# Mixer's feature products, K's sums and ScalarE's settling steps in another order, and a finer signal for the gathers

## The reference

```
q, k, v = feat @ Wq, feat @ Wk, feat @ Wv            # N x 4 heads x 64
e = (k[src] * q[dst]).sum(-1) / 16                   # for each edge and head
ft2 = segment_sum(v[src] * softmax_over_dst(e), dst)

qn, kn = normalize(q') * (scale * temperature), normalize(k') * scale    # 8 heads x 32
vN = concat([1, v']) / N
kv_mod = einsum('bhni,bhnj,bhne->bhije', kn, kn, vN)
kv, vsum = einsum('bhnd,bhne->bhde', kn, vN), vN.sum(-2)
y = 0.5 * einsum('bhni,bhnj,bhije->bhne', qn, qn, kv_mod) + scale**2 * (qn @ kv) + scale**4 * vsum
out = (y[..., 1:] / y[..., :1]) @ Wproj.T + bproj
```

## Time and profile before

| | us |
|---|---|
| median of 3 runs | 2665.03 |
| lowest and highest | 2663.69, 2670.76 |
| the profiled execution | 2674.8 |
| its span, first to last instruction | 2673.1 |
| mean granted share of TensorE's clock | 0.845 |
| edges and mixer, about | 110 to 1800 |

### The profile page before, as it was taken

How to read it: one execution, slowest core, us unless ns; L and a number is a source line. 1 busy time by engine, 2 the same in 40 slices (tenths; PEclk the granted TensorE clock), 3 DMA queues, 4 the chain that set the end, 5 groups by cost and what they waited for, 6 DMA issues and landing times. The chain is left out here.

```text
span 2673.1 us, 45626 instructions
## 1 busy us (share of the span) xinstructions
PE 2071.7 (78%) x12642; PEld 1468.3 (55%) x12642; DVE 1745.4 (65%) x3439; ACT 1496.3 (56%) x4918; POOL 1213.7 (45%) x1183
## 2 busy tenths in 40 slices
PE   7757767678767657777777777765989986999998
PEld 4323332223323245555555555544778875999997
DVE  7367676767667675566666656676989996444443
ACT  2256556566556535565665655665875544555554
POOL 0455555555565545455455545542840001444443
PEclk9878788888888857788777777786999997999999
DMA  7666566666665655566556556545950017322221
GB/s 214 207 193 187 171 182 181 188 182 183 190 191 169 188 152 170 173 177 182 171 174 187 168 166 189 175 148 174 312 161 23 31 34 258 69 33 35 33 35 22
DMA packets 227731, 406.06 MB, mean 152 GB/s; under 512 B 58972, under 2 KB 129809, under 8 KB 227521
## 3 DMA queue, kind: packets, MB, share of 16 engines
q0 software_dynamic: 83712, 250.84, 33.7%
q1 hardware_dynamic: 120852, 116.88, 14.7%
q10 hardware_dynamic: 22957, 35.95, 3.7%
HBM read 345.66 MB, written 58.83 MB: 151 GB/s over the span
## 5 line engine op out<-in xcount | busy, mean ns | idle before, releaser
L825 POOL DMA_INDIRECT ring<-kv_tab,idx x904 | 915.4, 1013 | 769.5 <-ACT val L1160 449.8
L1160 ACT ACTIVATE val<-ring,val 128x64 f32<-128x64 f32 x1808 | 475.5, 336 | 15.5 <-DVE part L927 5.9
L921 DVE TENSOR_TENSOR val<-val 128x1040 f32<-128x1040 f32 x113 | 140.4, 1242 | 294.4 <-ACT val L1160 284.8
L884 DVE TENSOR_TENSOR ring<-ring,tile_bank 128x1024 f32<-128x1024 f32 x226 | 273.9, 1212 | 27.5 <-ACT tile_bank L1150 23.4
L1275 PE MATMUL tile_bank<-q_win,spread 128*128 128x256 f32 x452 | 180.7, 487 | 114.5 <-DVE val L913 68.9
L889 DVE TENSOR_REDUCE score<-ring 128x16 f32<-128x1024 f32 x226 | 267.7, 1208 | 0.0
L1308 PE MATMUL bank_f<-pair,u_T 96*125 96x496 bf16 x200 | 94.3, 471 | 180.7 <-ACT u_T L697 55.0
L2226 POOL DMA_INDIRECT out<-e_yw,to_row x56 | 120.8, 2157 | 222.0 <-DVE e_yw L2253 205.6
L2302 PE MATMUL e_h<-e_xT,e_now 128*128 128x128 f32 x1792 | 211.8, 277 | 0.7 <-DVE e_now L2243 0.7
L2302 PEld LDWEIGHTS e_h<-e_xT,e_now 128*128 128x128 f32 x1792 | 207.0, 194 | 1.2 <-DVE e_now L2243 1.1
L1308 PEld LDWEIGHTS bank_f<-pair,u_T 96*125 96x125 bf16 x200 | 29.4, 147 | 322.6 <-issue 122.0
(11 more groups left out here) (423 smaller groups left out, 4956.3 us busy)
## 6 DMA issues: line engine op xcount, KB each, us to landing
g_ring<-parts SPq DMA_DIRECT2D x137, 260.0 KB, 4.3
parts<-part ACTq DMA_DIRECT2D x113, 260.0 KB
q_win<-q_tab SPq DMA_DIRECT2D x226, 128.0 KB
e_w_all<-L_ffn_W SPq DMA_DIRECT2D x16, 1024.0 KB, 11.7
ring<-kv_tab,idx POOLq DMA_INDIRECT x904
kv_tab<-kv_t SPq DMA_DIRECT2D x25, 224.0 KB
blocks<-t SPq DMA_DIRECT2D x216, 5.0 KB
blocks<-t SPq DMA_DIRECT2D x216, 0.0 KB
```

The source lines that it names most:

```text
L825: pool.indirect_dma_start(out=ring[:, n % RING, g * L + e, :], out_offset=None, in_=t.kv_tab, in_offset=bass.IndirectOffsetOnAxis(ap=idx[n ...
L884: dve.tensor_tensor(k, k, bcast(q_ps[g].unsqueeze(1), 128, L, F), ALU.mult).then_inc(q_read[g], 1)
L921: dve.tensor_tensor(v[:, :, 0:2 * FD], v[:, :, 0:2 * FD], v[:, :, 2 * FD:], ALU.add).then_inc(folding, 1)
L1160: one = act.activation(val[n % 2][:, 1, e, h, 0:DG], ring[:, n % RING, L + e, F + h * DG:F + (h + 1) * DG], ACT.Copy, scale=val[n % 2][:, ...
```

## The change

1. TensorE, feature products. k_first and q_first are renamed k_pairs and q_pairs and issued at the end of the micro step before, behind k_last or q_last. K's product gets a second PSUM tile (bank_f2), and waits for the square of head k - 2 where it waited for that of head k - 1.
2. K's sums. The Gram product leaves PSUM accumulation: each half of K (128 columns) is multiplied with V and with itself into one tile of bank_t, and VectorE adds both parts into SBUF (slv_acc and gram_sum). The order of the sums becomes ones, K squared, first half, second half, at k = 0, 2, 4, 5 on TensorE and 1, 3, 5, 6 on VectorE.
3. ScalarE's order. settle_rows moves from the end of quarter 1 to quarter 2 behind the square, settle_nodes from there to quarter 3 behind exps and mix_last.
4. Gathers. ScalarE signals each weighed slot of the second row set, and GpSimd waits for each slot before that slot's gather; VectorE's fold waits for the fourth.

```diff
-        kf_ps = bank_f[0:TP, 0:NPAIR]
+        kf_ps = [b[0:TP, 0:NPAIR] for b in (bank_f, bank_f2)]
-        gram_ps = bank_f2[:, 0:2 * 128].rearrange("p (a n) -> p a n", a=2)
+        both_ps = bank_t[:, 0:HW + 128]
+        gram_sum = qT[0].rearrange("p a k n -> p (a k n)")[:, 0:2 * 128].rearrange("p (a n) -> p a n", a=2)
...
                 for g in range(G):
-                    wait(pool, (val_ready, act_val_ready)[g], n - RING + 1)
-                    pool.sem_inc(carrier, 1)
+                    if g == 0:
+                        wait(pool, val_ready, n - RING + 1)
+                        pool.sem_inc(carrier, 1)
                     for e in range(L):
+                        if g == 1 and n >= RING:
+                            pool.wait_ge(act_val_ready, (n - RING) * L + e + 1)
+                            pool.sem_inc(carrier, 1)
...
-                dve.wait_ge(act_val_ready, n + 1)
+                dve.wait_ge(act_val_ready, (n + 1) * L)
...
+                dve.wait_ge(slv_ready, u * 4 + kind + 1)
+                wait(dve, slv_read, u * 4 + kind)
+                if kind < 2:
+                    parts = 1 if kind == 0 else 128
+                    at = x.slv_acc[0:parts, 2 if kind == 0 else 0, :, :]
+                    dve.tensor_tensor(at, at, slv_ps[0:parts, :, :], ALU.add).then_inc(slv_read, 1)
+                else:
+                    at = x.slv_acc[:, 1, kind - 2, :]
+                    dve.tensor_tensor(at, at, both_ps[:, 0:HW], ALU.add)
+                    at = gram_sum[:, kind - 2, :]
+                    dve.tensor_tensor(at, at, both_ps[:, HW:], ALU.add).then_inc(slv_read, 1)
...
-                if u >= 0 and k in (2, 4, 6):
-                    add_sums(u, k // 2 - 1)
+                if u >= 0 and k in (1, 3, 6):
+                    add_sums(u, k // 2)
...
+                    if kind == "k" and u >= 0 and k == 5 and stretch == 0:
+                        add_sums(u, 2)
...
-                        act.activation(phi_k[k % 2], kf_ps, ACT.Square).then_inc(kphi_ready, 1)
+                        act.activation(phi_k[k % 2], kf_ps[k % 2], ACT.Square).then_inc(kphi_ready, 1)
...
                     if c == 2 and n + AHEAD < TILES:
-                        settle_nodes(n + AHEAD)
+                        settle_rows(n + AHEAD)
...
                     mix_last(last)
+                    if c == 3 and n + AHEAD < TILES:
+                        settle_nodes(n + AHEAD)
...
-                    if c == 1 and n + AHEAD < TILES:
-                        settle_rows(n + AHEAD)
...
+                    half = kind - 2
+                    unit = k_.unit[u % 2][:, half * 128:(half + 1) * 128]
+                    pe.matmul(both_ps[:, 0:HW], unit, v1[u % 2][:, 4 * half:4 * half + 4, :].rearrange("p h e -> p (h e)"), start=True, stop=True)
+                    mm = pe.matmul(both_ps[:, HW:], unit, unit, start=True, stop=True)
                 mm.then_inc(slv_ready, 1)
...
-                    wait(pe, kphi_ready, u * HM + k)
-                    pe.matmul(kf_ps, k_.turned_parts[u % 2][:, k, 0:TP], x.pair3[:, :], start=True, stop=True).then_inc(kf_ready, 1)
+                    wait(pe, kphi_ready, u * HM + k - 1)
+                    pe.matmul(kf_ps[k % 2], k_.turned_parts[u % 2][:, k, 0:TP], x.pair3[:, :], start=True, stop=True).then_inc(kf_ready, 1)
...
+                if u >= 0 and k in (0, 2, 4, 5):
+                    kind = (k + 1) // 2
+                    wait(pe, slv_read, u * 4 + kind)
+                    sums(u, kind)
...
                 if u >= 0 and k < HM:
+                    wait(pe, qphi_ready, u * HM + k - 1)
...
+                for kind, u, k in micro_steps_of(i + 1):
+                    if kind == "k":
+                        k_pairs(u, k)
+                    elif kind == "q":
+                        q_pairs(u, k)
```

More of the change, by code:

```diff
@@ L728, in stage_edges_and_mix @@
         ring = t.ring
-        blocks, NBUF, IOTAS = x.blocks, AHEAD + 1, 6 + 2 * G
+        blocks, NBUF, IOTAS = x.blocks, AHEAD + 1, 7 + 2 * G
         q_win = [s.sb(f"q_win{i}", [128, G, F]) for i in range(2)]
@@ L1070, in _ @@
             dve.memset(gram, 0.0).then_inc(iotas, 1)
+            dve.memset(gram_sum, 0.0).then_inc(iotas, 1)
             dve.memset(t.marks[:, 0, :, :], -1.0).then_inc(iotas, 1)
@@ L1161, in weigh_slot @@
                                          scale=val[n % 2][:, 1, e, h, DG:])
-                if e == L - 1:
-                    one.then_inc(act_val_ready, 1)
+                one.then_inc(act_val_ready, 1)
             def keep_part(n):
@@ L1286, in sums, with k_pairs @@
             def sums(u, kind):
-                parts = 1 if kind == 2 else 128
-                for half in range(2):
-                    lhsT = (t.ones[0:TP, 0:1] if kind == 2 else
-                            (ksq[u % 2] if kind == 0 else k_.unit[u % 2])[:, half * 128:(half + 1) * 128])
-                    mm = pe.matmul(slv_ps[0:parts, half, :], lhsT, v1[u % 2][:, 4 * half:4 * half + 4, :].rearrange("p h e -> p (h e)"),
-                                   start=True, stop=True)
-                mm.then_inc(slv_ready, 1)
-            def gram_sums(u, half):
-                at = slice(half * 128, (half + 1) * 128)
-                pe.matmul(gram_ps[:, half, :], k_.unit[u % 2][:, at], k_.unit[u % 2][:, at], start=False, stop=(u == NT - 1),
-                          skip_group_check=True)
-            def k_first(u, k):
+                if kind < 2:
+                    parts = 1 if kind == 0 else 128
+                    for half in range(2):
+                        lhsT = t.ones[0:TP, 0:1] if kind == 0 else ksq[u % 2][:, half * 128:(half + 1) * 128]
+                        mm = pe.matmul(slv_ps[0:parts, half, :], lhsT, v1[u % 2][:, 4 * half:4 * half + 4, :].rearrange("p h e -> p (h e)"),
+                                       start=True, stop=True)
+                else:
+                    half = kind - 2
+                    unit = k_.unit[u % 2][:, half * 128:(half + 1) * 128]
+                    pe.matmul(both_ps[:, 0:HW], unit, v1[u % 2][:, 4 * half:4 * half + 4, :].rearrange("p h e -> p (h e)"), start=True, stop=True)
+                    mm = pe.matmul(both_ps[:, HW:], unit, unit, start=True, stop=True)
+                mm.then_inc(slv_ready, 1)
+            def k_pairs(u, k):
                 if u >= 0 and k == 0:
@@ L1325, in k_last @@
                 if k == 7 and u + 1 < NT:
-                    wait(pe, slv_read, 3 * (u + 1))
+                    wait(pe, slv_read, 4 * (u + 1))
                     k_.pe_turn(pe, u + 1, t.identb).then_inc(k_.turned, 1)
@@ L1373, in project, with q_pairs @@
                 mm.then_inc(out_ready, 1)
-            def q_first(u, k):
+            def q_pairs(u, k):
                 if u >= 0 and k == 0:
@@ L1413, in mix_first @@
                 for kind, u, k in micro_steps_of(i):
-                    if kind == "k":
-                        k_first(u, k)
-                    elif kind == "coef":
+                    if kind == "coef":
                         coef(k)
-                    elif kind == "q":
-                        q_first(u, k)
             def mix_last(i):
@@ L1434, in _ @@
             pe.wait_ge(fixed, 2)
-            for sums_ps in (*gT_ps, bank_f2[:, 0:NPAIR]):
+            for sums_ps in gT_ps:
                 pe.matmul(sums_ps, beside[0:1, :], x.pair3[0:1, :], start=True, stop=False, skip_group_check=True)
```

15 lines of the change are left out of this document (3 added, 12 removed).

## The result

The changed kernel takes 2715.94 us, the kernel before on the same chip 2666.61: a ratio of 1.0177 [1.0124, 1.0229] (95% interval), slower by 47 us. The prediction was 2624 us in a range of 2575 to 2700, with 0.62 on faster. A second pair on another chip gave 2717.31 against 2672.52, 1.0183 [1.0115, 1.0251]. The profiled execution took 2724.74 us (span 2723.0), 9 us above its median.

What follows compares the result with a forecast made beforehand. No engine was full; the 15.0 us step was taken as waiting, TensorE and ScalarE handing work over in tight order, VectorE behind ScalarE. Terms -46 - 13 + 6 + 7 + 5 + 0 = -41 us from 2665 gave 2624, range 2575 to 2700.

Steps and rivals of the forecast that it cites:

- Part F: GpSimd's gathers: slot-by-slot waits start three of four earlier, nobody collects this; 0 us, bounds -10 and +10.
- Part A: ScalarE's two settling steps move later: 25% of 186 us idle time gained, -46 us; bounds 0 and -93.
- Part B: K's feature product a step ahead on TensorE hides waits for squares: -13 us; bounds 0 and -40.
- Part C: K's sums on VectorE: four additions per tile for three, 18 us more, a third counted: +6; bounds 0 and +18.
- Part D: TensorE's fourth pair of K's sums waits for VectorE one quarter closer: +7 us; bounds 0 and +28.
- Part E: VectorE's times_q(n, 1) waits for node settling, now behind exps and mix_last: +5 us; bounds 0 and +81.
- rival 1: Slower: VectorE's second product waits behind ScalarE's unit work in 18 places, +81 for +5 us; 2700 us; chance 0.22.
- Rival 2: No change: TensorE sets the pace with its work and holds; Parts A and B give 0 to -10; 2662 us; chance 0.15.
- rival 3: Larger gain: TensorE and ScalarE come apart properly, Part A -93, Part B -27; -102 us in all, 2563; chance 0.13.

Runs made afterwards that it cites:

- b_settle: Kernel before with only ScalarE's new settling order (settle_rows in quarter 2, settle_nodes at the end of quarter 3): 0.9876 of before, chip 5.
- s_split1: Kernel before with the new settling order and row set 0's gathers waiting also for ScalarE's second weighed slot: 0.9657 of before, chip 3 (before 2293.7 us).
- b_split1: Kernel before with row set 0's gathers waiting also for ScalarE's second weighed slot: 1.0016 of before, chip 14, without holds.
- a_oldgather: Changed kernel with the old gathers back (one signal for all four slots of row set 1): 0.9881 of before, chip 5.
- b_mixer: Kernel before with only the second product buffer and K's sums by VectorE: 1.014 of before, chip 14, without holds.
- b_gather2: Kernel before with only the slot-by-slot signals for the second row set's gathers, on chip 3, without holds: 1.0012 of before.
- b_split1b: Same kernel as b_split1 (row set 0's gathers wait also for ScalarE's second weighed slot), on chip 12, with holds: 0.9855 of before.
- b_paced: Kernel before, but GpSimd issues one gather of each row set per slot that ScalarE has weighed: 0.9838 of before, chip 0.

## Why the prediction was wrong, by its own steps

**Part F is the step that failed: counted 0 (-10 to +10), measured 3.6% of 2695, +97 us alone and about +80 in the changed kernel.** It said that GpSimd's waiting for ScalarE would shrink from 449.8 us, and it did, to 206.9; it said that nobody collects the earlier landings, which also holds: VectorE waits for one once, 1.0 us. What it didn't ask was what else meets a gather that starts earlier. GpSimd's whole idle time ahead of the gathers grew all the same, from 769.5 us in the earlier trace rows to 818.7; what took the place of the named wait is called "issue", 598.8 us for 312.8, and with the updates that the trace lacks that may be ScalarE too. And the sentence behind it was "I take such holds as TensorE's own time, which no reordering of its neighbours removes". The earlier trace rows showed the holds; the row of gathers under them was in the same timeline and was not read. That sentence put the one neighbour that matters out of the sum. The test that it named at its end, that it is wrong "if the holds become more in number", came true: 95 for 82.

**Part A: right in kind, and in size as far as the runs tell.** -46 us predicted, b_settle gives -1.24%, -33 us, with an interval of -52 to -15 that has the -46 in it. The idle time ahead of the two settling lines fell from 186 us to 21.3 + 25.7 = 47 (forecast under 40); that ahead of the squares rose from 177.7 to 290.6 in K and from 221.1 to 281.7 in Q, 174 us in all (forecast under 140), and ahead of L697 from 67.2 to 108.6. But F is in that. With the settling order alone (b_settle) the squares' idle time is 247.2 and 263.3 us, 112 us more than in the kernel before, as forecast. Of ScalarE's 186 us 33, or 18%, came through, where 25% was taken. On a chip without holds the same edit was worth more: 0.9657 with it, 1.0016 without (s_split1 and b_split1, two chips), 3.6%.

**Part B: as read.** TensorE no longer waits for a square at the product; what is left of idle time there is 28.2 us for the 180.7 before, of it 12.4 for the turned K. The wait moved to the products into bank_g and bank_o, 79.7 us (53.3 + 9.8 + 16.6) for 8.3, more than the 40 that were forecast. TensorE's groups in the K half, two of before and then five of after:

```profile
L1308 PE MATMUL bank_f<-pair,u_T 96*125 96x496 bf16 x200 | 94.3, 471 | 180.7 <-ACT u_T L697 55.0 <-ACT phi L1193 49.7 <-issue 46.5
...
L1321 PE MATMUL bank_o<-xn_buf,v 125*32 125x496 f32 x100 | 53.5, 618 | 8.3 <-ACT xn_buf L1193 8.3
```

```profile
L1323 PE MATMUL bank_f<-pair,u_T 96*125 96x496 bf16 x200 | 92.2, 461 | 28.2 <-issue 15.7 <-ACT u_T L697 12.4
L1335 PE MATMUL bank_g<-xn_buf,v 125*32 125x496 f32 x100 | 68.7, 778 | 53.3 <-ACT xn_buf L1206 36.9 <-issue 16.4
L1335 PE MATMUL bank_o<-phi,v 125*32 125x496 f32 x100 | 65.1, 740 | 9.8 <-ACT phi L1206 8.3 <-issue 1.5
L1335 PE MATMUL bank_g<-phi,v 125*32 125x496 f32 x100 | 60.5, 692 | 16.6 <-ACT phi L1206 9.2 <-issue 7.4
...
L1311 PE MATMUL bank_t<-v,u_unit 125*128 125x132 f32 x100 | 30.0, 391 | 45.4 <-DVE xn_buf L975 20.4 <-issue 15.1 <-DVE slv_acc L970 9.8
```

**Part C: the arithmetic was exact.** VectorE's additions in the K half:

```profile
L970 DVE TENSOR_TENSOR slv_acc<-slv_acc,bank_t 1x264 f32<-1x264 f32 (+1 forms) x50 | 20.8, 415 | 45.9 <-remote 43.8 <-issue 1.8 <-PE bank_t L1306 0.3
...
L973 DVE TENSOR_TENSOR slv_acc<-slv_acc,bank_t 128x132 f32<-128x132 f32 x50 | 14.3, 287 | 17.5 <-remote 17.0 <-issue 0.5
L975 DVE TENSOR_TENSOR xn_buf<-xn_buf,bank_t 128x128 f32<-128x128 f32 x50 | 14.1, 283 | 0.0
```

20.8 + 14.3 + 14.1 = 49.2 us for the 31.3 of the earlier trace rows, +17.9 where +18 was worked out; 287 and 283 ns where 290 and 280 were interpolated. Two of three microseconds were taken as hidden, and here all of it was, as far as the runs tell. The Trainium skill (VectorE: DVE Perf Modes, "The TRN2 errata") led to 0.26 us for such an instruction; the rows say 0.28.

**Part D: a wait where it was expected, and longer.** TensorE waits 20.4 us in 12 times for L975 with a longest of 8.0, within the bound of 28 but not within its 1.1 us each. That B, C and D together come to nothing, as predicted (-13 + 6 + 7 = 0), holds to about 1% on the chip with holds (b_settle and a_oldgather, 0.9876 and 0.9881). On the chip without, b_mixer costs 1.4%, 32 us. Its waits of TensorE in the K half (110 to 950 us):

```profile
PE tile_bank L1286 <- DVE val L914: 61.0, 43, 3.1
PE bank_t L1308 <- DVE xn_buf L971: 24.5, 17, 2.6
...
PE bank_t L1303 <- DVE slv_acc L966: 11.6, 8, 1.5
```

24.5 + 11.6 = 36.1 us for the additions, where b_gather2, with the old sums, has 10.3; the loss is 32 us. VectorE is the busiest engine there (593.2 of 664 us, 89%, in b_split1's K half), so the 18 us of part C and the wait of part D can be paid in full; no run parts them from B. And B has little to give: TensorE waited for squares at the product only 16.7 + 3.8 = 20.5 us in b_gather2, for the 79 of the earlier trace rows. What the idle time of the earlier trace rows was worth, and what the earlier trace rows left free on VectorE, depended on the holds.

**Part E: within its price.** VectorE's wait for the node settling is 18.5 us in 3 times in Q (above), and 0.3 us once in K; over 40 was to prove rival 1. Rival 2 had part of the truth in its holds, rival 3 none.

**The sum, again with what was measured:** A alone -33 us, B to D 0, F alone +97: +64 us, or 0.9876 x 1.036 = 1.023, where the total is 1.0177 (+47 us; the medians are 49 us apart). A and F were measured on chip 5, the total on the first, and the intervals overlap. The +80 us for F in the changed kernel is no check of this: it was worked out from the total.

## What to carry to other kernels

Ahead of an edit that starts a transfer earlier, ask two questions: who waits for it, and what else runs at the time to which it moves. A wait that ends in "remote", or results of an engine that become usable microseconds after its instructions ended, are things to explain before the sum is made: lay the rows of transfers beside them, count how many fell in the last 10 us, and see where in the step they fall. And where holds of this sort stand in a trace, a small edit wants a second chip, since the same one was +3.6% on one and nothing on the other.

## What the runs showed of the hardware

**TensorE's signals can come microseconds late while GpSimd issues a row of gathers.** On chips 5 and 12 and the first, seven or eight indirect gathers of 128 rows in 10 us stood beside a held share of 0.62 to 0.91; with three or fewer it was about none (before). A hold ends a median 1.52 us after the row. Then the pending updates come one behind the other, a median 0.04 us apart, although their instructions ended up to 9 us apart. TensorE is not alone in it: under the hold of the earlier trace rows SyncE's own steps begin about 0.7 us apart from 588.41 to 592.66, where a register move of its takes a median 0.03 us outside the holds. Halving the bytes changes nothing (444 us held for 476). The Trainium skill (Perfetto Trace Analysis, "Tensor Engine Instruction (MATMUL, LD_WEIGHTS)") says that a matmul's recorded end is an estimate and that the semaphore is pushed only when PSUM has acknowledged the write; the trace agrees that the record proves nothing about when a result is usable: 10.0 us lie between them in the timeline above. Its page DMA: Bandwidth & Descriptors ("Why a DMA increments its semaphore by 16 and not by 1") says that each such gather has 16 engines post an increment whatever its shape. That would fit a cost that goes by number and not by bytes; no run here separates the increments from the descriptors, and the path of the delay stays open. A rival was not tested either: on these chips the trace loses about half of the stage's updates (12,756 for 26,124, above), and every time on record comes with a recorded span and clock, so no run tells whether the recording takes part in the holds.

**Chips differ.** Two of those used run the kernel before at 2290 us, the others at 2665 to 2695, 16 to 18% more, with the same code. The short ones have no hold with 20 gathers in a row, and TensorE, busy 648 of 780 us there and 562 with holds, has a granted clock of 0.88 for 0.81, both a mixture of 1.2 and 2.4 GHz. What makes a chip hold was not found.

**Spreading has a cheap form.** One more condition on the first set's gathers (b_split1b) brings about what interleaving all eight does (b_paced): 0.9855 and 0.9838, on two chips with holds.
